# Moving one chunk of node sums in front of the dense group's z, one between its remainder products, and the addition of the first sums on VectorE

## The reference

```python
h = relu(layernorm(x))
msg = relu(concat([h[dst], edge_attr]) @ W1a + b1a) @ W1b + b1b     # one row of 64 per edge
summed = segment_sum(msg, src, 6250)
agg = summed / maximum(counts, 1)[:, None]
out = x + relu(concat([h, agg]) @ W2a + b2a) @ W2b + b2b
```

## Time and profile before

| what | value |
| --- | --- |
| median of 3 runs | 1632.61 us (1630.75 to 1633.25) |
| profiled execution | 1626.88 us, its span 1625.0 us |
| TensorE (PE) | 1478.5 us busy, 91% |
| its weight loads (PEld) | 1400.4 us, 86% |
| VectorE | 1416.8 us, 87% |
| ScalarE | 1047.7 us, 64% |
| GpSimd | 1205.2 us, 74% |
| chain that ended last | PE 73%, ACT 11%, issue 5%, DMA 5%, DVE 3%, POOL 2% |
| granted TensorE clock | full (1.00) between 120 and 1560 us |

### The profile page before, as it was taken

One profiled execution on the slowest core, in us unless ns is written; L12 is line 12 of the kernel. 1 busy time (PEld: TensorE's weight loads), 2 busy tenths in 40 slices (PEclk: granted clock), 3 DMA queues, 4 the chain that ended last, 5 costly groups with the idle time before them and its releaser, 6 DMA issues.

```text
span 1625.0 us, 77131 instructions
## 1 busy us (share of the span) xinstructions
PE 1478.5 (91%) x31132; PEld 1400.4 (86%) x31132; DVE 1416.8 (87%) x4789; ACT 1047.7 (64%) x2192; POOL 1205.2 (74%) x794
## 2 busy tenths in 40 slices
PE   4378999999999999999999999999999999999946
PEld 3257999999999999999999999999999999899934
DVE  7857988989989899988898988988889989889947
ACT  5167766666666767666666667766666767666503
POOL 5166777788778788777787788787777878777771
PEclk9689999999999999999999999999999999999977
DMA  5666776767767677666677766776767767667651
GB/s 174 239 118 99 122 106 107 122 107 108 120 105 118 111 113 119 105 115 109 105 123 106 118 108 109 122 109 107 115 110 118 113 105 125 104 113 109 95 118 58
DMA packets 279402, 187.16 MB, mean 115 GB/s; under 512 B 190543, under 2 KB 275404, under 8 KB 278281
## 3 DMA queue, kind: packets, MB, share of 16 engines
q1 hardware_dynamic: 174070, 152.93, 39.5%
q0 software_dynamic: 104976, 29.30, 27.7%
HBM read 147.94 MB, written 34.17 MB: 112 GB/s over the span
## 4 chain that ended last, share of the span: by engine, by line
PE 73%; ACT 11%; issue 5%; DMA 5%; DVE 3%; POOL 2%; DVEq 0%; SPq 0%; POOLq 0%; ACTq 0%
PE l_ps L1257 31%; PE l_ps L1243 22%; PE z_ps L1207 8%; ACT area L701 7%; PE z_ps L1219 5%; PE c_ps L1231 5%; DMA sums<-vv,sidx 3%; ACT r_d L684 3%; PE z_ps L1212 2%; POOL sums L524 1%; DMA area<-sums 1%; DMA xs<-in_x 1%; DVE rank L873 1%; ACT r_s L684 0%; DVE area L857 0%
## 5 line engine op out<-in xcount | busy, mean ns | idle before, releaser
L524 POOL DMA_INDIRECT sums<-vv,sidx x726 | 1157.5, 1594 | 359.6 <-issue 169.7
L1257 PE MATMUL l_ps<-area 128*128 128x64 bf16 (+1 forms) x21000 | 793.0, 193 | 1.0 <-issue 0.4
L701 ACT ACTIVATE area<-l_ps 64x392 bf16<-64x392 f32 x1400 | 688.1, 491 | 127.4 <-PE l_ps L1243 97.1
L1257 PEld LDWEIGHTS l_ps<-area 128*128 128x128 bf16 x21000 | 746.0, 98 | 22.8 <-issue 1.9
L1243 PE MATMUL l_ps<-r_d,oh 128*128 128x196 bf16 x4200 | 483.6, 250 | 16.0 <-issue 8.3
L952 DVE TENSOR_SCALAR area<-iota,local 128x640 bf16<-128x640 int16 x1400 | 475.4, 404 | 4.9
L1243 PEld LDWEIGHTS l_ps<-r_d,oh 128*128 128x128 bf16 x4200 | 334.5, 96 | 26.9 <-ACT area L701 12.2
L684 ACT ACTIVATE r_d<-z_ps 128x384 f32<-128x384 f32 x423 | 207.8, 491 | 196.5 <-PE z_ps L1219 182.2
L937 DVE TENSOR_SCALAR oh<-iota,rank 128x640 bf16<-128x640 int16 x846 | 281.7, 401 | 0.0
L959 DVE TENSOR_TENSOR dense<-l_ps,dense 128x325 f32<-128x325 f32 x280 | 137.8, 492 | 115.2 <-PE l_ps L1257 110.0
L917 DVE TENSOR_TENSOR r_s<-r_s 128x384 f32<-128x384 f32 x242 | 134.3, 555 | 4.1
(11 more groups left out here) (133 smaller groups left out, 737.0 us busy)
## 6 DMA issues: line engine op xcount, KB each, us to landing
ids_s<-ids SPq DMA_DIRECT2D x248, 192.0 KB
et_d<-in_e_t SPq DMA_DIRECT2D x143, 192.0 KB
ids_d<-ids SPq DMA_DIRECT2D x143, 192.0 KB
et_s<-in_e_t SPq DMA_DIRECT2D x124, 192.0 KB
sums<-vv,sidx POOLq DMA_INDIRECT x726
sums<-dense POOLq DMA_DIRECT2D x3, 1657.5 KB
wp_d<-p_table SPq DMA_DIRECT2D x286, 15.8 KB
wp_s<-p_table SPq DMA_DIRECT2D x248, 15.8 KB
```

The lines of the kernel that those rows point to most:

```text
L524: nc.gpsimd.indirect_dma_start(out=sums[t][:, :], out_offset=bass.IndirectOffsetOnAxis(ap=index, axis=0), in_=rows, in_offset=None, comput ...
L701: ins = nc.scalar.activation(routed[on, t.div(MACRO).mod(2), first:second + 1:second - first, t.mod(MACRO), :], bank[on, :, :], ACT.Copy)
L1257: ins = nc.tensor.matmul(l2_ps[h][:, u * W:u * W + w], oh2[:, g, u * P:(u + 1) * P], rows[:, PARTS[r]:PARTS[r] + w], start=g % MACRO == 0 ...
```

## The change

TensorE's chunks are placed differently within the cycle. Chunks 2 and 3 no longer both stand between routes 2 and 3: chunk 3 goes behind route 3. Chunk 4 goes from there to behind z of the next dense group. So one chunk less stands in front of z. In front of the first remainder product there are still two chunks behind z (4 and 5 in place of 5 and 6), between the two products there are three (6, 7 and 8) in place of two. Chunk 4 now comes behind route 4 and z, so VectorE's addition of chunks 0 to 4 goes behind the route masks and the `hot` masks of the next dense groups.

```diff
@@ fast(), cycle on VectorE
                         if n and (s.per or s.base + 1 < SPARSE):
                             split_rows(s.plus(1))
-                        if sums_too:
-                            add_sums(now, 0)
                         if routes:
                             slots(t.plus(1))
                             hot(DN, t.plus(2))
+                        if sums_too:
+                            add_sums(now, 0)
                         if now.per or -1 <= now.base < DENSE - 1:
                             locals_of(now.plus(1))
                             nodes(now.plus(1), 0)
@@ cycle on TensorE
-                    for f, chunks in enumerate(((0,), (1,), (2, 3), (4,), ())):
+                    for f, chunks in enumerate(((0,), (1,), (2,), (3,), ())):
                         if routes:
                             route(t, f)
                         sums_of(*chunks)
                     if routes:
                         z(DN, t.plus(1))
-                    sums_of(5, 6)
+                    sums_of(4, 5)
                     if routes:
                         take_off(DN, t.plus(1), 0)
-                    sums_of(7, 8)
+                    sums_of(6, 7, 8)
                     if routes:
                         take_off(DN, t.plus(1), 1)
                     sums_of(9)
```

## The result

| comparison | before, median | changed, median | ratio (95% interval) |
| --- | --- | --- | --- |
| first | 1629.68 us | 1633.51 us | 1.0033 (1.0016 to 1.0049) |
| again, `r2_after` | 1619.28 | 1626.80 | 1.0052 (1.0034 to 1.0071) |
| again, `s2_after` | 1630.40 | 1635.06 | 1.0024 (1.0006 to 1.0043) |
| again, `r_after` | 1615.35 | 1600.39 | 0.9925 (0.9897 to 0.9952) |

The forecast was 1641 us, 8.4 us (0.51%) above the median shown. The first comparison gave 0.33% more, 5.4 us; the two medians themselves differ by 3.8 us. The direction was right, the size too large; and one later comparison went the other way, by a mechanism that no rival names. The profiled execution of the changed kernel took 1634.85 us (span 1633.1), 8.0 us more than that of before.

What follows compares the result with a forecast made beforehand. TensorE was taken to set the pace, losing time where ScalarE's chain is late. 108 sparse cycles at +0.033 us and 21 plain at +0.233 gave +8.4 us, 1641 us on the median; range 1618 to 1650.

Steps and rivals of the forecast that it cites:

- What bounds the kernel: Steady stretch: TensorE sets the pace and loses time where ScalarE's chain of evictions and z's split is late.
- GpSimd no longer waiting for L929: GpSimd's wait for VectorE's index: if it stops altogether, the end no longer follows TensorE; a sign of being wrong.
- (a): Chunks moved around the first remainder product: 0.45 us less TensorE work in front, 0.45 more behind, alone zero.
- (b): Routes 3, 4 and ScalarE's chain start earlier; second product 0.04 us later in one sparse cycle, 0.01 earlier in one plain.
- the late handovers: Starts of evictions 3 and 4 behind their routes: up to 1.12 us instead of 0.76, kept as they were.
- rival 1: Evictions 3 and 4 start promptly, a late semaphore being covered: all prompt -13.5 us, 1619 us; chance 0.18.
- (c): Second product over 129 cycles: 108 sparse at +0.033 us, 21 plain at +0.233 us, sum +8.4 us.
- counts in full: End of the program: the shift accumulated until GpSimd's last index wait at 1472 us reaches the end, later shift not.
- Rival 2: No change: mean handover falls between, sparse cycles gain 0.04 us each and pay for the others; 1632.6 us; chance 0.20.
- (d): VectorE's addition moves behind the masks: its wait disappears, costed at nothing, at most 0.5 us a cycle without cover.
- Rival 3: VectorE's later addition delays masks so chunk 0 or 5 waits, up to 0.2 us a cycle: 1658 us; chance 0.04.
- Rival 4: ScalarE's chain doesn't hold the first product: it moves the full 0.45 us, gain 8 us, 1625 us; chance 0.07.

Runs made afterwards that it cites:

- r2_after: The changed kernel, unedited, timed once more against the kernel before, with late handovers: 1626.80 us, ratio 1.0052.
- s2_after: The changed kernel, unedited, timed once more against the kernel before, with late handovers: 1635.06 us, ratio 1.0024.
- r_after: The changed kernel, unedited, timed once more against the kernel before, with prompt handovers: 1600.39 us, ratio 0.9925.
- r_before: The kernel before, unedited, run again for a second profile; handovers prompt with its scatters running: 1612.40 us.
- e5: The kernel before without GpSimd's scatters, first occasion: 1537.75 us; the changed kernel without them then took 1554.56 us.
- e8: The changed kernel without GpSimd's scatters, second occasion, on the same chip as e7: 1554.41 us, a single run.
- e7: The kernel before without GpSimd's scatters, second occasion, on a chip that showed late handovers: 1539.25 us, a single run.

## Why the prediction was right or wrong

**What bounds the kernel: right, but for late handovers only.** TensorE with ScalarE's chain in front of the first product sets the cycle in the first profile; in `r_before` it is GpSimd. The profile of before held a hint. Six scatters at 1.9 us are 11.4 us a group, against 10.6 us for a cycle with a sparse group, so GpSimd catches up only in the cycles without; and it waited for an index for 36.4 us in all, 145 to 1570 us:

```profile
POOL sums L524 <- DVE sidx L929: 36.4, 12, 6.9
```

In `r_after` that is 10.1 us. The prediction had named this sign, GpSimd no longer waiting for L929, but not as a way to a gain.

**(a), (b), the shifts: right in kind.** Route 3 0.40 us earlier (forecast 0.39), route 4 0.34 (0.38 in the cycle that was read), in plain cycles the first product 0.21 (0.17), the second 0.22 later (0.23).

**(b), the late handovers: the step that failed.** The forecast took the late handovers of one trace over into the new order, those of evictions 3 and 4 at their old places and sizes, and its sum ends at the second product, with nothing lost behind it. Neither held. The late handovers of evictions 3 and 4 nearly vanished (0.19 and 0.16 us to 0.05 and 0.02), since these evictions now start right behind others and a late semaphore is covered: rival 1's mechanism. So in sparse cycles the first product came 0.47 us earlier, not 0.36, and waited 0.25 us, not 0.34, and the second came 0.06 us earlier, where 0.03 later was forecast. But split 1 became late instead (0.08 to 0.20), and behind the second product the next cycle started 0.09 us later (0.71 to 0.80 us; 0.62 to 0.68 in plain cycles). The net is +0.03 us, as forecast, by luck: two errors cancelled.

**(c), the sum: near for the profile, too large for the runs.** It gave +8.4 us, and the two profiled executions differ by 8.0. In the three comparisons with late handovers the cycles' own sums are 108 x 0.03 + 21 x 0.275 = 9.0, 108 x 0.042 + 21 x 0.217 = 9.1 and 108 x 0.011 + 21 x 0.247 = 6.4 us, and the profiled executions differ by 8.0, 9.5 and 5.9 us (in the third, means of two and two). So what the cycles lose does reach the end, as "counts in full" had it. From cycle 134 to the end it takes 156.5 us before and 154.8 after, 157.0 and 155.9 in the second, 155.2 and 156.9 before and 155.8 and 157.4 after in the third: nothing regular comes back there. The ratios give 5.4, 8.4 and 3.9 us, 1 to 4 us less than the cycles' sums. The mis-sized term is thus the loss per cycle: it was read from the handovers of one execution and taken for all of them, while the part with a sparse group alone came out as 0.03, 0.04 and 0.01 us in three pairs of executions. Why the ratios lie below what the profiled pairs show stays open; executions of one kernel differ by up to 14 us (1623.42 to 1637.50), and the first interval, 2.6 to 8.0 us, only just leaves out 8.4.

**The absolute time.** 1641 rested on a median of three runs, 1632.61; nine more brought it to 1629.68. That is 2.9 of the 7.5 us by which 1641 was too high; the other 4.6 are the size, 8.4 against the 3.8 between the medians. Rival 2's 1632.6 us lies nearest to the 1633.51 measured, but only because the median of before fell; the ratio is not that of no change.

**(d), VectorE: not confirmed.** Costed at nothing; alone it measured +0.23% (0.07 to 0.39), which reaches from next to nothing to the whole first difference. What belongs to TensorE's order for certain is the loss in the cycles without a sparse group: 8.66 us with VectorE's order alone, 8.94 with both. Rival 3's named trace, a wait of TensorE for VectorE, is as good as absent, 0.2 us once in the changed kernel.

**Rival 1's price was wrongly worked out.** "All prompt, -13.5 us" set prompt handovers in the new order against the old one with its late ones. With all prompt in both, the old order waits for nothing and the new one for 0.11 us a cycle: 15 to 17 us slower (`e5` to `e8`). Its place in the forecast's low end was not earned. The gain that did occur, 0.9925, came with prompt handovers in both orders and with GpSimd at the limit, so its likely mechanism is GpSimd's pace; that the new order quickens it is not shown.

**Rival 4** fell: the first product did move by 0.47 us, but in both orders it starts 0.05 us behind the end of the split, and the whole got slower.

## What to carry to other kernels

A wait that is covered moves to the next tight handover: price a reordering by which handovers become tight, not by the one wait that it removes. Work out a rival against a baseline under the same condition, since what makes the new order fast often makes the old one faster. And where a second engine runs within a few per cent of the pace setter, expect the sign of a small change to depend on which of the two is ahead; give a median of three runs the width that executions show.

## What the runs showed of the hardware

ScalarE's start behind a TensorE result is 0.39 us behind a single product's start and 0.75 behind a route's, but up to 1.1 us later when the result comes while GpSimd is some 0.4 to 1.5 us into an indirect DMA's instruction; such starts then mostly fall 1.3 to 1.6 us behind the scatter's start (815.44 against 813.95, 847.28 against 845.83), and the instruction itself takes 1.59 us on average. In the first trace none of the results that came in the first 0.3 us of a scatter was held back for over 0.02 us. This tie to the phase of the instruction speaks for the instruction rather than the transfers as the cause; no run takes away one without the other. TensorE's start behind the end of the first split was 0.05 us in every cycle of the first trace, scatter or not. Without scatters nothing is late. And the same program with the same scatters was seen once with no handover tied to them late (a few of 0.5 us at any phase remain, 3 to 4% of cycles), 10.45 in place of 10.51 to 10.67 us a cycle.

The Trainium skill, "SBUF — State Buffer", section "Who interferes with whom", says that TensorE and ScalarE never wait on anyone. That may hold for their ports; for the handover between them the measurement decides. In front of the first product it shows 0.40 us a cycle lost beside GpSimd's work: from route 4 to that product 2.74 us in the first trace, 2.34 without scatters (`e7`).
